# Attention scores made once and transposed, in place of two score passes and a row of maxima

## The reference

```python
scores = (einsum(q_r, k_r) + einsum(q_i, k_i)) / sqrt(16)        # 512 x 512 for each head
scores = where(causal, scores, -inf)
probs = softmax(scores, axis=-1)
out = concat(einsum(probs, v_r), einsum(probs, v_i))             # 32 columns for each head
x = x + out @ Wo
x = x + xattn(layernorm(x), ctx)      # "decoder heads": 16 x 16 scores for each token
x = x + ffn(layernorm(x))
```

## Time and profile before

| what | us |
|---|---|
| median of 3 runs | 826.6 (825.58 to 826.87) |
| profiled execution, own time | 829.26 |
| its span, first to last instruction | 827.4 |
| PE busy | 759.1 (92%) |
| DVE busy | 628.8 (76%) |
| POOL busy | 489.6 (59%) |
| ACT busy | 402.8 (49%) |

### The profile page before, as it was taken

The page is one execution under the profiler, slowest core; times in us unless marked ns, Lnnn a source line. Parts: engine busy times, 40 slices in busy tenths (PEclk is TensorE's granted clock), DMA queues, the critical chain, the costliest instruction groups (busy, mean ns, idle before and its releaser), DMA issues.

```text
span 827.4 us, 15883 instructions
## 1 busy us (share of the span) xinstructions
PE 759.1 (92%) x5563; PEld 520.8 (63%) x5563; DVE 628.8 (76%) x1225; ACT 402.8 (49%) x760; POOL 489.6 (59%) x452
## 2 busy tenths in 40 slices
PE   3688999999999999999999999999999998998997
PEld 2565655765566556666666666665766564587995
DVE  2544555457768998899879987999798879789873
ACT  5114555555555566545646573647464546541111
POOL 5000000031966799678958786878787888976541
PEclk9658999999999999999999999999999999999997
DMA  5886656866686668566646675667566760100001
GB/s 180 111 105 82 98 78 84 135 84 84 84 135 78 90 84 134 70 91 107 90 94 90 103 93 100 90 104 95 76 87 107 100 93 8 58 14 8 32 14 38
DMA packets 47980, 70.54 MB, mean 85 GB/s; under 512 B 4897, under 2 KB 22578, under 8 KB 47922
## 3 DMA queue, kind: packets, MB, share of 16 engines
q1 hardware_dynamic: 46898, 69.52, 56.1%
q10 hardware_dynamic: 1024, 0.26, 0.1%
HBM read 14.98 MB, written 4.19 MB: 23 GB/s over the span
## 4 chain that ended last, share of the span: by engine, by line
PE 58%; DMA 15%; DVE 13%; POOL 5%; issue 4%; ACT 2%; SPq 1%; DVEq 0%; ACTq 0%; POOLq 0%
PE misc L518 21%; DMA stack_k<-k_lo 14%; PE exp_bank L518 14%; PE acc_bank L518 9%; PE max_bank L518 9%; PE sum_bank L518 3%; POOL prod L1570 3%; DVE neg_max L1201 2%; DVE seg_max L1201 2%; DVE x L1296 2%; SPq L449 1%; POOL prod L311 1%; DVE head_scores L1213 1%; DVE head_out L1213 1%; DVE ln_raw L1179 1%
## 5 line engine op out<-in xcount | busy, mean ns | idle before, releaser
L927 ACT ACTIVATE probs<-exp_bank 128x512 f32<-128x512 f32 x320 | 188.4, 592 | 204.0 <-PE exp_bank L518 201.1
L1201 DVE TENSOR_REDUCE neg_max<-max_bank 128x1 f32<-128x512 f32 (+1 forms) x192 | 130.6, 683 | 93.0 <-PE max_bank L518 92.4
L1570 POOL TENSOR_TENSOR prod<-head_probs,ctx_sb 128x256 f32<-128x256 f32 (+1 forms) x100 | 185.1, 1882 | 2.2 <-POOL head_probs L1565 0.5
L518 PE MATMUL max_bank<-stack_k,stack_q 96*128 96x384 f32 (+3 forms) x512 | 158.2, 372 | 17.2 <-DMA stack_k<-k_lo 9.1
L518 PE MATMUL acc_bank<-probs,values 128*32 128x512 f32 (+3 forms) x1024 | 157.6, 445 | 4.6 <-ACT log_sum L938 2.6
L311 POOL TENSOR_TENSOR prod<-x1n,ctx_sb 128x256 f32<-128x256 f32 (+1 forms) x104 | 158.4, 1554 | 4.3 <-ACT x1n L887 4.3
L518 PE MATMUL sum_bank<-probs,ones 128*32 128x512 f32 (+3 forms) x1024 | 156.9, 442 | 0.0
L518 PE MATMUL exp_bank<-stack_q,stack_k 97*128 97x384 f32 (+3 forms) x512 | 150.0, 355 | 2.1 <-DVE wf_lo L1171 1.3
L1512 POOL TENSOR_TENSOR ln_var<-ln_mv,eps 128x4 f32<-128x4 f32 x21 | 4.5, 213 | 198.3 <-DVE ln_mv L1187 198.3
L518 PEld LDWEIGHTS exp_bank<-stack_q,stack_k 97*128 97x128 f32 x512 | 84.1, 194 | 56.2 <-issue 28.2
L1201 DVE TENSOR_REDUCE seg_max<-max_bank 128x4 f32<-128x512 f32 x128 | 86.7, 682 | 28.2 <-PE max_bank L518 27.0
(11 more groups left out here) (181 smaller groups left out, 1360.2 us busy)
## 6 DMA issues: line engine op xcount, KB each, us to landing
stack_q<-q_hi SPq DMA_DIRECT2D x64, 256.0 KB, 5.6
stack_k<-k_hi SPq DMA_DIRECT2D x64, 256.0 KB, 9.6
stack_q<-q_lo SPq DMA_DIRECT2D x32, 256.0 KB, 7.0
stack_k<-k_lo SPq DMA_DIRECT2D x32, 256.0 KB, 10.7
x_in<-in_x SPq DMA_DIRECT2D x9, 512.0 KB, 4.7
ctx_sb<-in_ctx SPq DMA_DIRECT2D x32, 128.0 KB, 3.3
x<-in_x SPq DMA_DIRECT2D x7, 512.0 KB, 10.1
out<-y_sb SPq DMA_DIRECT2D x5, 512.0 KB, 3.3
```

The costliest lines, as they stand in the source:

```text
L518: return nc.tensor.matmul(*args, **kw)
L927: nc.scalar.activation(probs[:, (UNITS * g + n) % PTR, :], exp_bank[n % 2][:, :], ACT.Exp, scale=SCALE).then_inc(exp_done, 1)
L1201: vec.tensor_reduce(o, v, axis=AX_X, op=ALU.max, negate=True).then_inc(max_taken, 1)
L1570: last = gp.tensor_tensor(pv_prod[:, COFF[j]:COFF[j + 1]].rearrange("p (q d k) -> p q d k", q=4, k=keys), head_probs[:, 4 * j:4 * j + 4, N ...
```

## The change

The scores are made once, with queries on the partitions (`score_unit`, three banks). DVE takes the row maxima as before, now one reduction for each piece of a unit. ACT takes the exponential straight from that bank, with the negated maximum as a per-partition bias and the row sum as a second output (`accum_out`); a unit of two pieces needs two instructions. PE then transposes the probabilities, four 128 x 128 pieces for each unit (`turn_unit`), three units later (`LAG = 3`), into `turn_bank`, and ACT copies them to `probs_t` (`keep_turned`). `attend` works on a whole group at once, in the next group's unit 3. The row sums are inverted by DVE, spread by ACT to 32 columns (`widen_inverses`) and turned by PE (`spread_inverses`). The second score pass, `sum_bank`, the row of maxima and its DMA are gone. The projection is one group ahead in place of three, with `SLOTS = 2`. SCALE moves from the exponential to `q_hi` and `q_lo`. The hardware loop is gone; all eight batches are written out.

```diff
-    SLOTS = 4
+    SLOTS = 2
+    LAG = 3
             def group(ahead):
                 b, n = divmod(g + ahead, NG)
                 return (b, n) if ok(i + b) else None
-            return {"C": group(0), "B": group(2), "A": group(3), "M": group(1), "N": group(-1)}
+            return {"C": group(0), "A": group(1), "N": group(-1)}
...
+            def score_unit(n, slot):
+                wait(pe, exp_done, n_unit.up() - 3)
+                bank = score_bank[(n_unit.total - 1) % 3]
+                parts, (col, count, step) = QUERY_UNITS[n]
+                for k, (h, blk, at, width) in enumerate(parts):
+                    mm(bank[:, at:at + width], stack_q[0:STACK, slot, h, blk * P:(blk + 1) * P],
+                       stack_k[0:STACK, slot, h, 0:width], start=(k == 0), stop=False, skip_group_check=True)
...
+            def turn_unit():
+                pe.wait_ge(exp_done, n_turned.up())
+                wait(pe, probs_kept, n_turned.total - 2)
+                unit = n_turned.total - 1
+                for j in range(NT):
+                    last = nc.tensor.transpose(turn_bank[unit % 2][:, j * P:(j + 1) * P],
+                                               probs[:, unit % RING, j * P:(j + 1) * P], ident[:, :])
+                last.then_inc(turned, 1)
...
+            def attend(group):
+                pe.wait_ge(probs_kept, UNITS * n_group.up())
+                wait(pe, acc_saved, n_group.total - 1)
...
+                        if st["C"]:
+                            if n == 0:
+                                pe.wait_ge(stacked, n_stack.up(16 * STACK_DMAS))
+                            score_unit(n, st["C"][1] % SLOTS)
+                        if st["A"] and n in (0, 1):
+                            if n == 0 and st["A"][1] == 0:
+                                pe.wait_ge(xt_ready, n_xt.up(CC))
+                            project_qk(st["A"][1], n)
+                        if st["N"] and n == LAG:
+                            attend(st["N"][1])
+                        if st["N"] and n < LAG or st["C"] and n >= LAG:
+                            turn_unit()
+                        if st["N"] and n == LAG + 1:
+                            spread_inverses()
+                        if g == 1 and ok(i - 1) and n == 2:
+                            output_projection(1)
...
+            def exponential(n, group):
+                act.wait_ge(max_taken, n_unit.up())
+                unit = n_unit.total - 1
+                wait(act, turned, n_unit.total - RING)
...
+                for h, blk, at, width in QUERY_UNITS[n][0]:
+                    last = nc.scalar.activation(probs[:, unit % RING, at:at + width],
+                                                score_bank[unit % 3][:, at:at + width], ACT.Exp,
+                                                bias=neg_max[:, ring, h, blk:blk + 1],
+                                                accum_out=row_sum[:, ring, h, blk:blk + 1])
+                last.then_inc(exp_done, 1)
...
+                        if st["N"] and n < LAG or st["C"] and n >= LAG:
+                            keep_turned((n - LAG) % UNITS)
+                        if st["A"] and n in (1, 2):
+                            act.wait_ge(qk_psum, n_qk.up())
...
+                        if st["C"]:
+                            exponential(n, st["C"][1])
```

More of the change, by code:

```diff
@@ L32, with __init__ @@
 class Count:
-    def __init__(self, turn, per_batch):
-        self.turn, self.per_batch, self.total = turn, per_batch, 0
+    def __init__(self):
+        self.total = 0
     def up(self, n=1):
         self.total += n
-        return self.now()
+        return self.total
     def now(self, back=0):
[L46 to L78, removed]
+        return self.total - back
 def wait(eng, sem, value):
-    if not isinstance(value, int) or value > 0:
+    if value > 0:
         eng.wait_ge(sem, value)
[L87 to L95, removed]
 def decoder_layer(nc, x, ctx_in, wq, wk, wv, wo, ffn_w, ffn_bias, ffn_a, ffn_b, out):
@@ L633, in output_projection, with spread_inverses @@
+            def spread_inverses():
+                pe.wait_ge(inv_spread, n_group.total)
+                bank = take(1, attn_ready, r_attn)
+                for t in range(NT):
+                    last = mm(bank[:, t * P:(t + 1) * P], inv_wide[:, t, :], ident[:, :], start=True, stop=True)
+                last.then_inc(inv_psum, 1)
             def output_projection(half):
-                bank = take(half, x1_added, r_x1)
+                bank = take(1 - half, x1_added, r_x1)
                 for t in range(2):
@@ L833, in _ @@
             pe.wait_ge(const_ready, 1)
-            turn.batches(pe, body, N_BATCH)
+            for i in range(-1, N_BATCH):
+                body(i)
             pe.wait_ge(setup_act, 2)
-            attend((8, 9), NG - 1, UNITS * (NG - 1))
+            for n in range(LAG):
+                turn_unit()
+            attend(NG - 1)
+            spread_inverses()
             last_projection_most()
@@ new lines, in keep_turned @@
+            def keep_turned(n):
+                act.wait_ge(turned, n_kept.up())
+                unit = n_kept.total - 1
+                if n == 0:
+                    wait(act, pv_done, unit // UNITS)
+                src = turn_bank[unit % 2][:, :]
+                place = turned_place(n)
+                if n < 2 * G:
+                    src = src.rearrange("p (b q) -> p b q", q=P)
+                else:
+                    src = src.rearrange("p (h b q) -> p h b q", b=2, q=P)
+                copy(place, src).then_inc(probs_kept, 1)
@@ L923, in body @@
                         if st["C"]:
[L925 to L928 removed]
+                            exponential(n, st["C"][1])
+                        if (i, g) == (-1, 3) and n == 3:
+                            other_weights()
```

595 lines of the change are left out of this document (240 added, 355 removed).

## The result

The changed kernel takes 930.1 us in the median (928.0 to 933.0), the kernel before 826.2: a ratio of 1.126, with an interval of 1.123 to 1.129. The forecast was 851 (792 to 895), so the direction was right and the size wrong by 79 us, outside the range.

The account below looks back on a forecast made before the run. PE set the pace, DVE close behind; after the change three engines stand at 76 to 78 a batch. Start 133.7, batches 1 to 6 539, batch 7 80, tail 99: span 852, median 851 us (792 to 895).

Parts of the forecast that it names:

- Start, tail and work: Start through batch 0 133.7 us, tail after the last group's `acc_sb` 99; per batch ACT needs 76.5, PE 78.
- The row sum's 0.1: ACT's row sum output taken as its own instruction, 0.1 us net each, x 64 = 6.4 us a batch.
- the 22 taken: Length of each group in batch 0: 20.4 us for stacking plus 1.6 for slower projections.
- the 20.4 that was called the least: Least group length: q's copy ends at 5.9 us, then 14.5 from q's high part through stacking DMAs to scores.
- rival 3: Stacking binds everywhere because q's copy is late: group 23.5 us, batch 94, about 870 us in all; chance 0.06.
- 14.6 us of waits in a batch: ACT's waits: 2.2 transposes behind projections, 3.5 attention, 5.9 output projection, 3 projection behind `values`; added to 76.5, batch 91.
- The walk: Following one group through the engines' queues, from unit 0's scores, to size the waits: 14.6 us a batch.
- the projection before the transposes: Units 0 and 1: a 1.5 us projection precedes a transpose on PE; ACT waits 0.55, x 4 = 2.2 a batch.
- Rival 2: TensorE's clock falls in the middle too: batch longer by about 7 us, total time 893 us; chance 0.09.
- The price of the row sum in the range: Batch of 85 us with the row sum free, 95.5 at its highest price, giving the range 815 to 878.
- Rival 1: The three-unit lag hides the waits and the kernel is faster: batch 82, about 790 us in all; chance 0.31.
- the terms of attention, of the output projection and of v: ACT's waits a batch: attention 3.5 us after filling, output projection 5.9, projection behind the copy of `values` 3.

Follow-up runs that it names:

- c3_both: Changed kernel with GpSimd's first-normalisation coefficients behind the heads' work of group 0, and TensorE's transposes ahead of the projections in units 0 and 1: 856.7 us.
- experiments 1 and 2: Changed kernel with GpSimd's first-normalisation coefficients moved to group 0's end (897.2 us), or VectorE's statistics of x_in moved to units 1 and 2 (896.4 us).
- experiment 3: Changed kernel with TensorE transposing the unit's probabilities before projecting q and k in units 0 and 1: 891.8 us.
- f1_fill: c3_both with useless TensorE matmuls at the end of units 5, 6 and 7 of group 1 in seven batches: 846.2 us.
- d3_all: c3_both with VectorE's reciprocal writing the spread inverses and v's second projection moved from group 0 to group 2: 903.2 us.
- d2_v2: c3_both with v's second projection moved from units 6 and 8 of group 0 to units 2 and 4 of group 2: 888.9 us.
- d1_dvewiden: c3_both with VectorE's reciprocal writing the inverses spread over 32 columns, without ScalarE's copy: 898.5 us.
- d5_dvecopy: d1_dvewiden with the reciprocal of 16 elements as before and a VectorE copy that spreads it: 853.4 us.
- f2_v2fill: d2_v2 with useless TensorE matmuls in units 5, 6 and 7 of groups 0 and 1: 897.5 us.
- f3_afterfill: Changed kernel with useless TensorE matmuls in units 5 to 8 of groups 0 and 1: 950.0 us.
- g2_fill01: d5_dvecopy with useless TensorE matmuls in units 5, 6 and 7 of group 1 and units 2 and 5 of group 0: 860.9 us.

## Why the prediction was right and wrong

- **Start, tail and work: right.** 131.0 against 133.7, 98.1 against 99; ACT's work in a batch 75.1 against 76.5, PE's 83.2 against 78 (part of it at half clock; c3_both has 79.5). The row sum's 0.1 was right. Batch 0's groups were 22.6, 19.6 and 22.8 long, about the 22 taken, though one is under the 20.4 that was called the least. PE waited for the stacking 3.9 and 2.4 us in two of them. From batch 2 on it never did for more than 0.8: rival 3 is out.
- **The step that failed: 14.6 us of waits in a batch.** It came to about 26, as batches 1 to 6 took 101.7 each on average and not 91, with ACT's work as forecast. The walk followed PE, ACT and VectorE. It never passed through POOL's queue, where `ln_coefficients(0)` stands ahead of the heads' products and now waits for statistics that VectorE takes in units 5 and 7 of the same group. That term was put at nothing. It is some 7 us in each of batches 2 to 6, 33 us in all (experiments 1 and 2).
- **A term mis-sized: the projection before the transposes**, 2.2 a batch. It measured 5.3 in batches 1 to 6 and 38 over the run, some 23 us more than the walk's 2.2 in seven batches (experiment 3). The walk counted ACT's wait, not q's high part behind it nor VectorE's wait for that. (Two of the walk's sums are off by 0.02 and 0.05: 4.85 should be 4.83, and 2.95 should be 2.9. Nothing hangs on it.)
- **Rival 2, the clock, was real and small.** Its sign was there, PEclk under 9 in middle slices. It priced 42 us; the runs show 10.5, measured on c3_both, in one stretch of each batch. The clock falls behind the places where PE waits, so it comes with the other two and is not in place of them. The page cited there ("TensorE: Matmul & The Clock Gate", Part 4, of the Trainium skill) says that transposes don't count as activity as matmuls do, and the prediction took from it a deeper fall. The traces show no such fall: with 40 transposes in every group f1_fill's batches 4 to 6 run at 1.00 throughout, and so do groups 2 and 3 of the changed kernel in batch 4. Whether transposes count is left open by that, as other matmuls stood among them.
- **The price of the row sum in the range**: free, it was to save 6 a batch. It saves 2.4 in each of batches 1 to 6 and 18.8 in all. The forecast's premise that a batch is ACT's work plus ACT's waits is too simple, since much of what ACT is spared turns into waiting.
- **Rival 1** (lag of three units hides the waits) is out: even with both orders mended and the clock held a batch takes 90.3.
- **Not settled.** 33 + 23 + 10.5 = 67 of the 79 us. For the other 12 there are the terms of attention, of the output projection and of v; none was measured alone on the changed kernel. ACT idles 4.07 us before its copy in unit 3 of group 1, behind half an output projection and attention, and 0.5 in group 0, behind attention alone; moving the other half of the output projection was worth 16 us on d3_all. Of d2_v2's 32 us the wait for `k_lo` can hold 15; the rest is open. A second buffer for `probs_t`, which might take away the wait for attention, wasn't tried; it takes another 32 KB of each partition (4 x 4 x 512 f32).

## What to carry to other kernels

When a change moves an engine's work to another group, walk every in-order queue that the moved instructions pass, also of engines with half their time free: here four POOL instructions of 0.2 to 1 us cost 33 us by waiting in front of 8 us of work that others wanted. Two orders of independent work on one engine are worth a run each, since it is the item that another engine's queue stands behind that has to go first. And where PE's idle time is spread over waits, compare the clock of stretches with the same work before believing that less work is faster.

## What the runs showed of the hardware

- **A reciprocal on VectorE costs 6.25 ns a column**: 243 ns for 16 columns (c3_both) and 3344 for 512 (d1_dvewiden), where a maximum over 512 takes 681. A copy of the 16 spread to 512 took 783 (d5_dvecopy), so the small reciprocal with a copy is 2.3 us cheaper.
- **An addition on VectorE stands still while GpSimd multiplies.** In c3_both, timelines of VectorE and of GpSimd (the last of its four products):

```profile
491.29 3.00 DVE L1213 TENSOR_TENSOR x<-x,head_out 128x256 f32<-128x256 f32 x1
```

```profile
491.08 2.92 POOL L1469 TENSOR_TENSOR prod<-head_probs,ctx_sb 128x1024 f32<-128x1024 f32 x1
```

  This addition takes 0.41 us in the median, and 0.42 in the changed kernel at 430.17, where GpSimd stands still. Here it starts 0.21 after GpSimd's product and ends at 494.29, 0.29 after it (494.00), and ACT then waits 2.44 for the maximum queued behind it. VectorE's reductions ran beside the products before it at their usual length. The kernel before has long additions of this kind too, of up to 2.5 us. In d2_v2 it is the same, 2.85 us, in the very stretch that did not shorten when matmuls were taken out of it; that this pinned the stretch is argued, not shown. The Trainium skill ("SBUF — State Buffer", "SBUF: two separate sides") says that a VectorE operation with two SBUF inputs and a GpSimd one that reads SBUF exclude each other for a whole instruction; the trace agrees.
- **More work for TensorE can mean less time, and mostly doesn't.** Added matmuls brought 10.5 us in one stretch, whose clock rose from 0.86 to 1.00 (f1_fill), and cost 9 to 20 in three other kernels (f2_v2fill, f3_afterfill, g2_fill01); why they cost as much there is not shown.
